# Shared expert: the gelu's result stays in its PSUM bank instead of going to an SBUF tile

## The reference

```python
def _L0_ffn_ref(x, gate_w, gate_b, w1, b1, w2, b2, ws1, bs1, ws2, bs2):
    logits = xf @ gate_w + gate_b
    top_w, top_i = jax.lax.top_k(logits, K)
    gw = jax.nn.softmax(top_w, axis=-1)
    combine = (gw[:, :, None] * jax.nn.one_hot(top_i, E)).sum(axis=1)
    for e in range(E):
        h = jax.nn.gelu(xf @ w1[e] + b1[e], approximate=False)
        out = out + combine[:, e:e + 1] * (h @ w2[e] + b2[e])
    shared = jax.nn.gelu(xf @ ws1 + bs1, approximate=False) @ ws2 + bs2
    return (out + shared).reshape(orig_shape)
```

## Time and profile before

| | |
|---|---|
| time of 3 runs | 634.68 us median, 632.59 to 636.75 |
| profiled execution | 635.94 us, span on the core 634.2 us |
| busy: PE, DVE, ACT, POOL | 483.8, 508.8, 454.5, 371.9 us |
| mean granted TensorE clock | 0.924 of full |
| shared expert, layer 0 and layer 1 | about 141 to 226 us and 431 to 494 us of the span |

### The profile page before, as it was taken

How to read it: one execution, slowest core, us unless ns; L and a number is a source line. 1 busy time by engine, 2 the same in 40 slices (tenths; PEclk the granted TensorE clock), 3 DMA queues, 4 the chain that set the end, 5 groups by cost and what they waited for, 6 DMA issues and landing times.

```text
span 634.2 us, 13564 instructions
## 1 busy us (share of the span) xinstructions
PE 483.8 (76%) x3827; PEld 358.1 (56%) x3827; DVE 508.8 (80%) x1181; ACT 454.5 (72%) x826; POOL 371.9 (59%) x391
## 2 busy tenths in 40 slices
PE   6788217774891988999677688875998879998770
PEld 6333017762440467888566577753444669997650
DVE  5899898888884448999788699876986479997992
ACT  2688995967592758999667577847797678997650
POOL 7000093337877778777667321147787777777673
PEclk9999858996796899999989999978999999999896
DMA  8810000004334644545741115101445435547943
GB/s 267 243 39 1 1 0 1 1 22 134 94 95 114 122 106 95 98 107 103 179 97 49 61 65 135 34 26 34 135 117 122 107 89 107 103 102 140 229 133 126
DMA packets 116798, 60.76 MB, mean 96 GB/s; under 512 B 81332, under 2 KB 105912, under 8 KB 116728
## 3 DMA queue, kind: packets, MB, share of 16 engines
q1 hardware_dynamic: 107640, 41.14, 28.6%
q0 software_dynamic: 9088, 18.76, 10.5%
HBM read 16.29 MB, written 23.90 MB: 63 GB/s over the span
## 4 chain that ended last, share of the span: by engine, by line
issue 25%; DVE 19%; SPq 18%; POOL 17%; PE 11%; ACT 6%; DMA 3%; POOLq 0%; DVEq 0%; ACTq 0%
POOL routed_rows L808 12%; SPq L630 11%; SPq L639 4%; SPq L628 2%; PE PA L1254 2%; DVE big L2160 2%; DMA side<-expert_results 2%; DVE side L2174 2%; ACT SC L1012 1%; PE PC L1472 1%; DVE BN L1492 1%; POOL RS L733 1%; DVE X L1697 1%; ACT big L1012 1%; DVE W L1620 1%
## 5 line engine op out<-in xcount | busy, mean ns | idle before, releaser
L857 POOL DMA_INDIRECT expert_results<-side,DG x156 | 163.1, 1046 | 58.6 <-issue 46.4
L808 POOL DMA_INDIRECT routed_rows<-big,SLQ x128 | 142.8, 1116 | 51.7 <-issue 39.4
L1472 PE MATMUL PC<-W,big 128*128 x624 | 119.0, 277 | 30.2 <-DVE side L2174 29.4
L1149 ACT ACTIVATE SC<-PA,B1T,scl 128x256 f32<-128x256 f32 x208 | 100.6, 573 | 16.4 <-PE PA L1456 12.1
L2163 DVE SCALAR_TENSOR_TENSOR big<-SC,scl,big 128x1024 f16<-128x1024 f32 x78 | 100.2, 1284 | 2.8
L1474 PE MATMUL PC<-W,big 128*128 x468 | 87.6, 222 | 0.0
L1472 PEld LDWEIGHTS PC<-W,big 128*128 128x128 f16 x624 | 58.5, 99 | 43.4 <-issue 35.6
L2160 DVE TENSOR_SCALAR big<-SC,scl 128x1024 f16<-128x1024 f32 x78 | 66.8, 856 | 5.9 <-ACT SC L1149 5.9
L1159 ACT ACTIVATE big<-PC,DG 128x128 f32<-128x128 f32 x156 | 49.8, 382 | 25.7 <-PE PC L1472 13.1
L733 POOL TENSOR_TENSOR RS<-VA,halfneg 128x4 f32<-128x4 f32 x24 | 25.3, 1055 | 64.5 <-DVE VA L1731 64.4
L2001 DVE SCALAR_TENSOR_TENSOR big<-SC,scl,big 128x1024 f16<-128x1024 f32 x32 | 41.0, 1282 | 25.2 <-ACT big L1119 24.8
(11 more groups left out here) (289 smaller groups left out, 1179.9 us busy)
## 6 DMA issues: line engine op xcount, KB each, us to landing
big<-PB SPq DMA_DIRECT2D x32, 256.0 KB, 3.3
side<-expert_results SPq DMA_DIRECT2D x16, 512.0 KB, 4.1
routed_rows<-pad_zeros SPq DMA_DIRECT2D x23, 128.0 KB
expert_results<-side,DG POOLq DMA_INDIRECT x156
X<-n_L_attn_a_hidden_states SPq DMA_DIRECT2D x2, 1024.0 KB, 7.0
W<-in_L_ffn_w SPq DMA_DIRECT2D x1, 2048.0 KB, 8.5
routed_rows<-big,SLQ POOLq DMA_INDIRECT x128, 2.6
out_x<-X SPq DMA_DIRECT2D x8, 256.0 KB
```

The source lines that it names most:

```text
L808: pool.indirect_dma_start(routed, bass.IndirectOffsetOnAxis(ap=SLQ[:, slot, t, c:c + 1], axis=0), XHL[:, slot, t, c, :].bitcast(I32), None ...
L857: pool.indirect_dma_start(results, bass.IndirectOffsetOnAxis(ap=DG[:, k, r, 0:1], axis=0), YT[:, k, r, :], None).then_inc(result_stored[k] ...
L1149: ins = act.activation(HF[:, k % 3, b * RU:(b + 1) * RU], up_out(k, b), ACT.Gelu, scale=INV1, bias=B1T[:, bass.ds(b1_at + b, 1)])
L1472: last = pe.matmul(both, hh, W2[:, :, at], start=(b == 0), stop=(b == HB - 1))
```

## The change

`shared_gelu` writes its result over its own input in `PA[n % 2]`. Both halves of the split then read the PSUM tile instead of SC. The semaphore that counts the gelu is a new one, `h_gelu`; the tile's own semaphore `a_read`, for which up(n + 2) waits, is now raised by the end of DVE's low part, and not by the end of the gelu. The semaphore of the low part, `hl_ready`, goes: `shared_down` waits for `a_read` of both tiles instead, and the waits that kept SC from being overwritten go too, or move behind the shared expert. No engine's instructions change their order or number, only operands and waits do.

```diff
 def shared_gelu(n, h, k, early=False):
     act.wait_ge(s["h1_ready"], m + 1)
-    wait(act, s["hl_ready"], m - 3)
     for b in range(2):
         col = E * HB + 2 * (k % 2) + b
-        ins = act.activation(HF[:, k, b * GT:(b + 1) * GT], PA[k % 2][:, b * GT:(b + 1) * GT],
-                             ACT.Gelu, scale=INV1, bias=B1T[:, col:col + 1])
-    ins.then_inc(a_read[k % 2], 1)
+        half = PA[k % 2][:, b * GT:(b + 1) * GT]
+        ins = act.activation(half, half, ACT.Gelu, scale=INV1, bias=B1T[:, col:col + 1])
+    ins.then_inc(s["h_gelu"], 1)
...
 def early_gelu(n):
-    if layer:
-        for g in (NG - 2, NG - 1):
-            act.wait_ge(a_read[g % 2], lin_read("kv", g))
-            act.wait_ge(c_read[g % 2], lin_read("q", g))
     shared_gelu(n, 0, n, early=True)
...
 def shared_hi(n, h, k):
-    act.wait_ge(a_read[k % 2], read("A", f"shared{layer}", k % 2, g))
+    act.wait_ge(s["h_gelu"], layer * NA + n + 1)
     act.activation(HH[:, slot, 2 * (k % 2):2 * (k % 2) + 2, :],
-                   HF[:, k, :].rearrange("p (b t) -> p b t", b=2), ACT.Copy,
+                   PA[k % 2][:].rearrange("p (b t) -> p b t", b=2), ACT.Copy,
                    scale=SH).then_inc(s["hi_ready"], 1)
...
 act.wait_ge(s["table_ready"], layer + 1)
-act.wait_ge(s["hl_ready"], (layer + 1) * NA)
+if layer:
+    for g in (NG - 2, NG - 1):
+        act.wait_ge(a_read[g % 2], lin_read("kv", g))
+        act.wait_ge(c_read[g % 2], lin_read("q", g))
...
 def shared_down(n, h, k, early=False):
-    pe.wait_ge(s["hl_ready"], m + 1)
+    for block in (n - 1, n):
+        pe.wait_ge(a_read[block % 2], read("A", sp_, block % 2, block // 2))
...
 def shared_split(n, h, k, early=False):
-    dve.wait_ge(a_read[k % 2], read("A", sp_, k % 2, 2 * h + k // 2))
+    dve.wait_ge(s["h_gelu"], layer * NA + n + 1)
     b = slice(2 * (k % 2), 2 * (k % 2) + 2)
-    hf = HF[:, k, :].rearrange("p (b t) -> p b t", b=2)
+    hf = PA[k % 2][:].rearrange("p (b t) -> p b t", b=2)
     if n < EARLY:
         dve.tensor_scalar(HH[:, slot, b, :], hf, SH, None, ALU.mult).then_inc(s["hh_ready"], 1)
     dve.scalar_tensor_tensor(HL[:, slot, b, :], hf, SH, HH[:, slot, b, :], ALU.mult,
-                             ALU.subtract).then_inc(s["hl_ready"], 1)
+                             ALU.subtract).then_inc(a_read[k % 2], 1)
```

More of the change, by code:

```diff
@@ L482, in build @@
             gap_ready th_ready routed_out_ready rows_ready
-            hi_ready cb_mixed cb_parts ct_turned0 ct_turned1 ct_turned2 ct_turned3 b2_loaded b2_steps scattered0 scattered1 scattered2 scattered3
+            hi_ready h_gelu cb_mixed cb_parts ct_turned0 ct_turned1 ct_turned2 ct_turned3 b2_loaded b2_steps scattered0 scattered1 scattered2 scattered3
             row_copied0 row_copied1 row_copied2 row_copied3
-            h1_ready hh_ready hl_ready y_ready y_copied y_turned
+            h1_ready hh_ready y_ready y_copied y_turned
             table_step table_ready pads_made pads_stored
@@ L1048, in gap @@
                     act.activation(TH[:, tiles], DD[:, tiles], ACT.Tanh, scale=0.5).then_inc(s["th_ready"], 1)
-                wait(act, s["hl_ready"], layer * NA)
                 wait(act, s["rhl_ready"], layer * UNITS)
@@ L1346, in shared_down @@
                         return
-                    slot, m = k // 2, layer * NA + n
-                    pe.wait_ge(s["hl_ready"], m + 1)
+                    slot = k // 2
+                    for block in (n - 1, n):
+                        pe.wait_ge(a_read[block % 2], read("A", sp_, block % 2, block // 2))
                     wait(pe, c_read[slot], used("C", sp_, slot) + h)
@@ L1989, in shared_split @@
                         return
-                    m, slot = layer * NA + n, k // 2
-                    dve.wait_ge(a_read[k % 2], read("A", sp_, k % 2, 2 * h + k // 2))
-                    g = 2 * h + k // 2
+                    slot, g = k // 2, 2 * h + k // 2
+                    dve.wait_ge(s["h_gelu"], layer * NA + n + 1)
                     wait(dve, s["y_ready"], layer * NG + g - 1)
                     b = slice(2 * (k % 2), 2 * (k % 2) + 2)
-                    hf = HF[:, k, :].rearrange("p (b t) -> p b t", b=2)
+                    hf = PA[k % 2][:].rearrange("p (b t) -> p b t", b=2)
                     if n < EARLY:
```

## The result

The changed kernel takes 627.5 us (median of 4 runs, 626.35 to 627.76) where the kernel before takes 634.01 on the same chip: ratio 0.9889, 95% interval 0.9852 to 0.9926, or 7.0 us less (4.7 to 9.4 by the interval). Its profiled execution takes 627.62 us with a span of 625.9, where the one before had 635.94 and 634.2.

A forecast was written before the change was run, and what follows sets the result against it. The chain was taken to pass POOL's scatters, stretched beside DVE's low part, then SP's queue into the routed units. Layer 0's -4.9 and layer 1's -0.9 make -5.8 us: 634.68 to 628.9, range 624.5 to 634.0.

The forecast's parts named there:

- What stretches the scatters: POOL beside DVE: a DVE instruction with two SBUF inputs holds scatters; freeing them saves 5.42 us (layer 0), 7.05 (layer 1).
- Layer 0: SP's gate turns, all behind them and POOL's last scatter start earlier: 5.42 - 0.5, so -4.9 us.
- The 0.5 for the early high part on POOL's path: Layer 0: one early high part lies ahead of the statistics POOL waits for, +0.5 us.
- Early high part: DVE, four times a layer: reading PSUM takes 1.28 us instead of 0.77, 0.51 more each; +2.0 in layer 1.
- Gelu and high part on ACT: ACT: gelu writing PSUM and high part reading it were taken as 0 us.
- The held bank: PE: up(n + 2) waits for DVE's low part; 0 in layer 0, in layer 1 low(8) 2.8 late, `table_ready` 2.9.
- an up that waits over 1 us for DVE in most pairs of blocks: PE's up-projections: a sign that would show the prediction wrong.
- Layer 1: Unit 3 waits no longer for scatters but for SP and DVE, which start 2.9 us later: -0.9 us.
- layer 1 gives more: Rival: early parts cost little or the bank wait hides; up to 3.8 us in layer 1, 626.0; chance 0.13.
- The table late by more: Rival, layer 1: costlier early high parts and bank waits make `table_ready` 5.3 us late, 631.3; chance 0.19.
- Scatters not freed: Rival: something other than the second SBUF input stretches POOL's scatters; 635.2 us, chance 0.07.
- Two banks don't suffice: Slower rival, layer 1: blocks 4 to 10 each pay a full low part, `table_ready` 10.8 late; 636.8 us, chance 0.05.

The follow-up runs named there:

- the release alone: Against the kernel before: gelu and both halves stay in SBUF, only the bank's release moves to the low part's end; 634.74 us, ratio 1.0007.

## Why the prediction was right

*What stretches the scatters.* Right, as far as it goes. One operand, from SBUF to PSUM, is 8.9 us. SBUF — State Buffer of the Trainium skill, "Who interferes with whom", states beside the clause that the prediction set aside that a VectorE instruction with two SBUF inputs contends with a GpSimd instruction that reads SBUF, and that the one that comes second stands still until the first is done. The traces agree where the scatter, which takes its list from SBUF, comes second: it needs most of its 0.96 us after the low part's end (0.82 to 0.98). Where the low part comes second, they show no standstill. Before the change one starts 0.06 us after a scatter, and both take their usual time:

```profile
190.35 0.96 POOL L808 DMA_INDIRECT routed_rows<-big,SLQ  x1 [0.31 <-issue]
```

```profile
190.41 1.29 DVE L2001 SCALAR_TENSOR_TENSOR big<-SC,scl,big 128x1024 f16<-128x1024 f32 x1 [0.92 <-ACT big L1119]
```

Within 0.10 us of the low part's start it can go either way: with the release alone, the scatter at 191.39 takes 0.96 and the low part of 191.30 beside it 1.35, while the scatter at 196.44, 0.01 after a low part's start, takes 2.09.

The prediction's rule, two SBUF inputs, is too narrow. An instruction with one tensor input stretches a scatter as well, here a TENSOR_SCALAR from SBUF: three scatters before the change start in the middle of a high part made by DVE (L1997, L2160) and take 1.20 to 1.43. One of them, POOL then DVE:

```profile
507.43 1.43 POOL L808 DMA_INDIRECT routed_rows<-big,SLQ  x1 [0.30 <-DVE side L2174]
```

```profile
507.29 0.74 DVE L2160 TENSOR_SCALAR big<-SC,scl 128x1024 f16<-128x1024 f32 x1
```

The same kind of instruction from PSUM, the early high part after the change, leaves the scatter its 0.96:

```profile
441.60 0.96 POOL L808 DMA_INDIRECT routed_rows<-big,SLQ  x1 [0.30 <-issue]
```

```profile
441.21 1.28 DVE L1994 TENSOR_SCALAR big<-PA,scl 128x1024 f16<-128x1024 f32 x1
```

*Layer 0.* Predicted -4.9 for the gate turns and all behind them; SP's turns came 5.11 earlier, PE's wait ended at 199.96 (predicted 199.86), layer 1 began 5.13 earlier, and layer 0 alone measures 5.0. That the end of the wait agrees to 0.1 is luck: the second profile of the same kernel has 198.48. Counted from layer 0's first scatter (145.99 before, 146.26 and 145.08 in the two profiles after) the wait ends 5.07 and 5.37 earlier. PE came to it 2.93 later (192.03 and 194.96), and the 5.00 us that are left cover that, as predicted. The 0.5 for the early high part on POOL's path was of the right size: POOL's wait for the statistics is 1.57 us instead of 0.52 and ends 0.53 later from the first scatter (9.10 and 8.57).

```profile
155.36 1.57 POOL L733 TENSOR_TENSOR RS<-VA,halfneg 128x4 f32<-128x4 f32 x1 [1.57 <-DVE VA L1729]
```

*Early high part.* Predicted 1.28 us, measured 1.277. The formula of VectorE: DVE Perf Modes of the Trainium skill, "The TRN2 errata", cited in the prediction, gave 1.19; the trace decides for 1.28. Four of them make the table some 2 us late: it follows layer 1's first scatter by 60.23 us after the change, by 58.36 with the release alone, and by 58.05 with the early blocks in SBUF.

*Gelu and high part on ACT.* Taken as 0, measured 23 and 36 ns less each. ScalarE: Activation LUTs of the Trainium skill, "Step-by-step: what each stage is for", cited in the prediction, says that ScalarE's writes to PSUM have the lower latency; the trace agrees for the gelu, 747 ns against 770.

*The held bank.* This term was of the right size, and the table hides it. As predicted, up(8) starts when low(6) ends (457.49 to 458.77), and low(8) then finds DVE idle for longer: 1.47 us where it was 0.53 before. With the release alone it is 1.52 (the last row), so the bank costs 0.9 to 1.0 here.

```profile
458.83 0.39 PE L1333 MATMUL PA<-QT,W1H 128*128 128x512 f16 x1 [0.55 <-DVE big L1998]
```

```profile
463.04 1.28 DVE L1998 SCALAR_TENSOR_TENSOR big<-PA,scl,big 128x1024 f16<-128x1024 f32 x1 [1.47 <-ACT big L1113]
```

```profile
467.69 1.28 DVE L2001 SCALAR_TENSOR_TENSOR big<-SC,scl,big 128x1024 f16<-128x1024 f32 x1 [1.52 <-ACT big L1118]
```

Yet with the release alone the table follows layer 1's first scatter by 58.36 us against 58.24 before. The kernel before had lost as much earlier, in its one profile. Where PE makes up(0) and the product (L1300) that DVE waits for, TensorE's granted clock was at half, the lower of its two levels (1.2 GHz), having fallen while PE was busy without a pause; after the change it was at full in that place. These are PE's windows, two before and then one after (length, busy (count), clock, DMA share, GB/s):

```profile
430.40:432.40 2.00, 2.00 (x10) 0.76 0.10 33
432.40:434.40 2.00, 1.91 (x8) 0.50 0.11 33
```

```profile
427.30:429.30 2.00, 1.63 (x11) 1.00 0.11 33
```

DVE waited for PE there before, and not after:

```profile
434.91 0.69 DVE L1798 TENSOR_TENSOR X<-PC,X 128x512 f32<-128x512 f32 x1 [0.92 <-PE PC L1300]
```

```profile
428.87 0.69 DVE L1796 TENSOR_TENSOR X<-PC,X 128x512 f32<-128x512 f32 x1
```

So block 0's high part starts 20.10 us after layer 1's first scatter before, and 19.2 in the other seven profiles in which DVE makes it. `table_ready` is 2.0 late against a profile that was itself 0.9 late, which makes the predicted 2.9. Whether other executions of the kernel before lose that 0.9 too stays open.

The prediction had named an up that waits over 1 us for DVE in most pairs of blocks as a sign against itself. Five ups of layer 1 wait for a low part after the change, three of them that long: up(2), up(11) and up(13). Beside up(8) above these are

```profile
435.13 0.61 PE L1333 MATMUL PA<-QT,W1H 128*128 128x512 f16 x1 [1.30 <-DVE big L1998]
451.58 0.39 PE L1333 MATMUL PA<-QT,W1H 128*128 128x512 f16 x1 [0.65 <-DVE big L1998]
468.11 0.39 PE L1333 MATMUL PA<-QT,W1H 128*128 128x512 f16 x1 [1.37 <-DVE big L1998]
475.56 0.39 PE L1333 MATMUL PA<-QT,W1H 128*128 128x512 f16 x1 [1.45 <-DVE big L1998]
```

*Layer 1.* Predicted -0.9, -2.1 in the profile up to unit 3. The mechanism was as written: unit 3 no longer waits for the scatters and its 3.78 us of idle time are gone. What it subtracted from them, 2.9, was too much for this profile: the table was 2.0 late, by the 0.9 above, and of that some more went into idle time ahead of unit 0's output, which the prediction didn't look at: DVE waited 2.98 us there for ACT before, and 1.39 after.

```profile
503.38 0.61 DVE L2171 SCALAR_TENSOR_TENSOR side<-PC,DG,big 128x128 f32<-128x128 f32 x2 [1.39 <-ACT big L1153]
...
511.19 0.61 DVE L2171 SCALAR_TENSOR_TENSOR side<-PC,DG,big 128x128 f32<-128x128 f32 x2
```

Unit 0's output is 3.38 earlier than before, that is 1.75 late against layer 0's 5.13, and 3.78 - 1.75 = 2.03 is what is left for unit 3 (2.1 measured). That is a fraction of the rival "layer 1 gives more" (up to 3.8), with the same cause. The measured time of layer 1 alone, 0.6 less, is nearer to the predicted 0.9 than to the profile's 2.1, and its interval (2.0 less to 0.8 more) holds the one and not quite the other.

*The rivals that fell.* The table late by more: 2.0, not 5.3. Scatters not freed: 0.19 of 6.04 us left. (The prediction's 7.05 for layer 1 leaves out 0.17 at 448.09, whose like at 165.41 it counts in layer 0; nothing hangs on it.) Two banks don't suffice: the release alone costs 1 us at low(8) and nothing in the time (1.0007), since unit 3 has more than that to spare.

The sum was 5.8 us, the gain is 7.0 (6.7 the second time). The predicted 628.9 stands 1.4 over the 627.5; half of that is the baseline, whose median is 634.01 with the fourth run and was 634.68 with three, and the other half lies within the interval.

## What to carry to other kernels

Where GpSimd issues indirect DMAs back to back and is on the chain, look at what VectorE runs beside each long one. Here an instruction with two SBUF inputs, or a TENSOR_SCALAR from SBUF in its fast form (1024 columns in 0.75 us), held a scatter that started in its middle until 0.8 to 1.0 us after its own end; with one input in PSUM the scatter was free, at no cost on VectorE where that instruction runs as fast from there. A freed microsecond counts only in the stage whose next limit lies further off, so size each stage by what becomes late next and not by the time that is freed. An instruction with one input that loses its fast SBUF form by the move (here 0.77 to 1.28 us) was better given to an engine with room.

## What was not expected of the hardware

- A float32 scale to float16 by DVE's TENSOR_SCALAR takes 0.772 us for 1024 columns from SBUF and 1.277 from PSUM, while SCALAR_TENSOR_TENSOR of the same size takes 1.28 us with either.
- A scatter that starts in the middle of VectorE's low part waits for it, while a low part that starts 0.06 us after a scatter takes its usual 1.29 us.
- PE waited up to 1.45 us for the bank in five ups of layer 1, and the time of the kernel with the release alone doesn't show it (1.0007).
- The read-back of results late in layer 1 makes DVE stand for 2.0 to 6.8 us in profiles of nearly the same program.
